# Gram products of a block computed in one go and kept in SBUF, per-couple element-wise work, expert weights applied to x, and a new instruction order

## The chip, the cores and the metric

The kernel runs on one core of a Trainium2 chip. The metric is the device time of one execution in microseconds (us), the median of three runs. One further execution was profiled; all rows below come from it, and their times count from the start of its span.

## The reference

The input x is (2 batches, 128 times, 16 bands, 64 channels). The reference first adds to x the result of six layers of a dual-path selective-state network (Mamba2) on a normed x, then adds a dense mixture of 16 experts. Each of the 12 passes (a "time" pass over t, then a "band" pass over the 16 bands, six times) computes, cut to what matters:

```python
zxbcdt = rmsnorm(x) @ Win
xBC    = silu(causal_conv4(xBC))            # xs (128), B (16), C (16)
dt     = softplus(dt + dt_bias)             # 8 heads
h_t    = exp(-dt*exp(A)) * h_{t-1} + (xs*dt) B_t ;  y_t = h_t . C_t + D*xs
x      = x + rmsnorm(y * silu(z)) @ Wout
# mixture of experts, top 2 of 16, all experts computed
out    = x + sum_e mix[:, e] * ((silu(x @ w1[e]) * (x @ w2[e])) @ w3[e])
```

The recurrence is evaluated without a scan. For a stretch of positions t and sources s it is y_t = sum_s G[s,t] * L[s,t] * dt_s * xs_s, with the Gram matrix G = B^T C, shared by the eight heads, and L = exp(cumsum differences) for each head.

## The kernel before

A pass is two blocks, one for each batch, so there are 24 blocks (k = 0 to 23), each 1024 positions with 128 inner channels. Block kind 0 is a time pass and kind 1 a band pass. A block has 8 pairs (i), two pairs make a couple (c = i // 2). In a pair the positions lie in halves of 64: kind 0 needs three (source, target) squares, LL, LH and HH; kind 1 needs two, LL and HH. All engines follow orders written out by hand, with semaphores between them; the work on block k is interleaved with the preparation of block n = k + 1.

For a pair, TensorE does these steps in order:

- `g_and_xt(n, i)`: the Gram products of the pair, from `bc` (B rows) and `cm` (C rows), 16 partitions each, into one PSUM bank `gx`, and two transposes of `xs` into the same bank. It waits for `s_w`: the weighing of the pair before must have read `gx` (lines 700 to 720).
- `mix_states(k, i)`: 32 small float32 products of `em` (weighted decays) and `xdt` into `ybank`, after `weigh(k, i)` (lines 733 to 749).
- `decays(n, i)`: the exponents L, as bf16 products of `lt` and `rt` into the ring of four PSUM banks, a bank a square (lines 722 to 731).

ScalarE takes each ring bank through `exps` (Exp) into `em`. VectorE does `x_dt` (transposed xs times dt), `weigh` (em times G, broadcast over heads, 128 x 1536 elements for kind 0, 128 x 1024 for kind 1) and `gate_y` (the skip D*xs from `ybank`, line 1252, and the gate, line 1262) for each pair, and `norm_out` for each couple. GpSimd squares the gated y for each pair (`square_y`, line 556) and adds the couple's output to x (`add_x`, line 563). `project_out(k, c)` on TensorE makes the output projection and the sum of squares.

The preparation of block n: `mean`, `project_dt`, `turn_dt`, `project_x` (8 products of 512 columns in two calls), `sum_dt`, `project_bc`, `project_z` and `turn_parts`. SyncE's queue then issues the DMAs in the order written: `c_rows(n)`, four DMAs that place the C rows (`cm`) once `bc` is ready (line 396), and `target_rows(n, 0)` and `(n, 1)`, together 12 DMAs for kind 0 and 8 for kind 1, which place rows of `rt` once `rows_of_cum` has copied the output of `turn_parts` to `lt` (line 407). `g_and_xt(n, 0)` waits for all four `cm` DMAs, `decays(n, 0)` for `target_rows(n, 0)`, and `decays(n, 4)` for `target_rows(n, 1)`. The order at the end of a block, before:

```python
# TensorE
project_x(n, 1); turn_parts(n); project_z(n, 0); project_z(n, 1)
project_out(k, 2); g_and_xt(n, 0); mix_states(k, 7); decays(n, 0); decays(n, 1)
# SyncE
c_rows(n); target_rows(n, 0); target_rows(n, 1)
```

In the expert stage there are 4 chunks of 512 columns and 16 experts, 64 steps. In each step TensorE computes h1 and h2 for two halves of the tokens (line 867), two bf16 products that spread the expert's mixing weight over the rows (line 872) and the output product (line 891). ScalarE applies Silu, and VectorE makes four products of 128 x 512: silu times h2, and that times the mixing weight, for two halves (lines 1409 and 1414).

Of the kernel before, what the change touches and what calls it, by code (L numbers as in the profile page):

```python
# [11 lines left out]
P = 128  # L12
QUAD = 32
# [71 lines left out]


def ring_turns():
# [12 lines left out]
    t.two("z", 0, 1)  # L100
    t.seg(0, 0)
    t.seg(0, 1)
    for k in range(NBLOCK):
        n = k + 1
        t.seg(k, 2)
        t.seg(k, 3)
        t.seg(k, 4)
        t.one("mean", n, 1)
# [5 lines left out]
        t.two("x", n, 0)  # L114
        t.one("cum", n)
        t.two("bc", n)
        t.two("x", n, 1)
        t.one("parts", n)
        t.two("z", n, 0)
        t.two("z", n, 1)  # L120
        t.seg(n, 0)
        t.seg(n, 1)
        t.one("mean", n + 1, 0)
    return t.turn


def build(nc, a, out):
    with ExitStack() as ctx:
# [8 lines left out]
        gx = ctx.enter_context(nc.psum_tensor("gx", [P, CK], F32))  # L137
# [3 lines left out]
        def rbank(*key):  # L141
# [53 lines left out]
        xdt = [sb(f"xdt{u}", [P, 2 * HEADS // 2, 2, 2 * HD]) for u in range(2)]  # L195
        yt = [sb(f"yt{u}", [P, 2 * T]) for u in range(2)]
# [29 lines left out]
        s_g, s_xdt, s_w, s_y, s_yf, s_yg, s_ysq = (sem(n) for n in (  # L226
            "g_and_x_turned", "xdt_ready", "weighed", "y_ready", "y_bank_read", "y_gated", "y_squared"))
# [9 lines left out]
        sil, act_h = ([emf[:, CK * (2 * k + b):CK * (2 * k + b + 1)] for b in range(2)] for k in range(2))  # L237
        hidden = [[emf[:, CK * (4 + 2 * k + b):CK * (5 + 2 * k + b)] for b in range(2)] for k in range(2)]
        moe = rstd[:, 0, :]
        xq = rstd[:, 1, :]  # L240
# [8 lines left out]
        target = [rt1[:, E * P * b:E * P * (b + 1)].rearrange("p (e t) -> p e t", e=E) for b in range(2)]  # L249
# [11 lines left out]
        s_xq, s_h1, s_h2, s_gb, s_sil, s_u, s_hid, s_eo, s_oc2, s_ot, s_acc = (sem(n) for n in (  # L261
            "xq_ready", "h1_ready", "h2_ready", "mix_spread", "silu_done", "silu_times_h2", "hidden_ready", "expert_out",
            "sum_copied", "sum_transposed", "accumulated"))
        NSTEP = 2 * E
        bank = ring + [gx, ybank[:, 0, :], ybank[:, 1, :], oss]
# [36 lines left out]
        def in_half(ap):  # L302
            return ap.rearrange("p (m w) -> p m w", w=HALF)

# [40 lines left out]
        def _(sp):  # L345
# [4 lines left out]
            def weights_in(g):  # L350
# [5 lines left out]
                if g >= 2:  # L356
                    sp.wait_ge(s_wp, g - 1)
                    sp.wait_ge(s_yg, NPAIR * 2 * (g - 1))
# [32 lines left out]
            def c_rows(n):  # L391
                sp.wait_ge(s_bc, 2 * (n + 1))
                if n >= 2:
                    sp.wait_ge(s_g, NPAIR * (n - 1))
# [24 lines left out]
            for k in range(NBLOCK):  # L419
# [11 lines left out]
            sp.wait_ge(s_yg, NPAIR * NBLOCK)  # L431
            sp.wait_ge(s_g, NPAIR * NBLOCK)
# [15 lines left out]
        def _(pool):  # L448
# [102 lines left out]
            def square_y(k, i):  # L551
                p, u = NPAIR * k + i, (i // 2) % 2
                pool.wait_ge(s_yg, p + 1)
                if p >= 4:
                    pool.wait_ge(s_o, p // 2 - 1)
                pool.tensor_tensor(out=ysq[u][:, i % 2, :], in0=yg[u][:, i % 2, :], in1=yg[u][:, i % 2, :],  # L556
                                   op=ALU.mult).then_inc(s_ysq, 1)
# [8 lines left out]
            for k in range(NBLOCK):  # L566
                for i in range(NPAIR):
                    square_y(k, i)
                    if i == 0 and k >= 1:
                        add_x(k - 1, 3)  # L570
                    if i == 3:
                        add_x(k, 0)
                    if i == 5:
                        add_x(k, 1)
                    if i == 6 and k % 2 == 0 and k >= 2 and pass_of(k) + 1 < NPASS:
                        weights_made(pass_of(k) + 1)
                add_x(k, 2)
            add_x(NBLOCK - 1, 3)
# [10 lines left out]
            for b in range(2):  # L589
                selector(pool.memset(target[b][:], 0.0))  # L590
                for r in range(NPART):
                    v = target[b][QUAD * r:QUAD * (r + 1)]
                    selector(pool.affine_select(out=v, in_=v, compare_op=ALU.not_equal, fill=1.0, base=-E * b,
                                                pattern=[[-1, E], [0, P]], channel_multiplier=1))

        @block.tensor
        def _(pe):
# [102 lines left out]
            def g_and_xt(n, i):  # L700

                p = NPAIR * n + i
                if i == 0:
                    pe.wait_ge(s_cm, 64 * (n + 1))
                    pe.wait_ge(s_xs, 4 * (n + 1))
                if p:
                    pe.wait_ge(s_w, p)
                rows = slice(QUAD * (i // 2), QUAD * (i // 2) + NST)
                b, c = (pair_of(t[n % 2][rows, :], i % 2) for t in (bc, cm))
                wide = T if kind(n) == 0 else HALF  # L710
                for ab in range(2):
                    pe.matmul(gx[HALF * ab:HALF * (ab + 1), 0:wide], b[:, 0, ab, :], c[:, 0:wide // HALF, ab, :],  # L712
                              start=True, stop=True)
                for ab in range(2):
                    pe.matmul(gx[HALF * ab:HALF * (ab + 1), wide:wide + HALF], b[:, 1, ab, :], c[:, 1, ab, :],
                              start=True, stop=True)
                for h in range(2):
                    tr = pe.transpose(gx[:, 2 * T + T * h:2 * T + T * (h + 1)],  # L718
                                      xs[n % 2][:, 2 * T * i + T * h:2 * T * i + T * (h + 1)], ident[:])
                tr.then_inc(s_g, 1)  # L720
# [12 lines left out]
            def mix_states(k, i):  # L733
                p = NPAIR * k + i
                pe.wait_ge(s_w, p + 1)
                if p:
                    pe.wait_ge(s_yf, p)
                wide = T if kind(k) == 0 else HALF
                for first in (0, 1):
                    lo, hi = (0, wide) if first == 0 else (wide, wide + HALF)  # L740
                    for r in range(2):
                        for q in range(HEADS // 2):
                            for ab in range(2):
                                rows = slice(HALF * ab, HALF * (ab + 1))
                                o = ybank[QUAD * q:QUAD * (q + 1), ab, (HALF if first else 0):(T if first else wide)]
                                mm = pe.matmul(o, xdt[p % 2][rows, 4 * first + q, r, :],  # L746
# [4 lines left out]
            def project_out(k, c):  # L751
                u, m = pass_of(k) % 2, 4 * k + c
                pe.wait_ge(s_ysq, NPAIR * k + 2 * c + 2)
# [24 lines left out]
            g_and_xt(0, 0)  # L778
# [3 lines left out]
            for k in range(NBLOCK):  # L782
                n = k + 1
                more = n < NBLOCK
                g_and_xt(k, 1)
                mix_states(k, 0)
                decays(k, 2)
                if k:
                    project_out(k - 1, 3)
                g_and_xt(k, 2)  # L790
                mix_states(k, 1)
                decays(k, 3)
                g_and_xt(k, 3)
                mix_states(k, 2)
                decays(k, 4)
                if more:
                    mean(n, 1)
                g_and_xt(k, 4)
                mix_states(k, 3)
                decays(k, 5)  # L800
                project_out(k, 0)
                if more:
                    project_dt(n)
                g_and_xt(k, 5)
                mix_states(k, 4)
# [3 lines left out]
                project_out(k, 1)  # L809
                g_and_xt(k, 6)  # L810
                mix_states(k, 5)
                decays(k, 7)
                if more:
                    project_x(n, 0)
                    sum_dt(n)
                    project_bc(n)
                g_and_xt(k, 7)
                mix_states(k, 6)
                if more:
                    project_x(n, 1)  # L820
                    turn_parts(n)
                    project_z(n, 0)
                    project_z(n, 1)
                project_out(k, 2)
                if more:
                    g_and_xt(n, 0)
# [30 lines left out]
            pe.wait_ge(s_sel, 2 * (1 + NPART))  # L857

            def chunk(q, first=False):
                def experts_in(e):  # L860
                    again = e >= 1 or not first
                    for w, k, used in ((w1s, 0, s_sil), (w2s, 1, s_u)):
                        for b in range(2):
                            if again:
                                pe.wait_ge(used, NSTEP * q + 2 * e + b - 1)
                            rows = slice(C * b, C * b + C)
                            pe.matmul(bank[2 * b + k][:], w[rows, e, :], xq[rows, :],  # L867
                                      start=True, stop=True).then_inc((s_h1, s_h2)[k], 1)
                    for b in range(2):
                        if again:  # L870
                            pe.wait_ge(s_hid, NSTEP * q + 2 * e + b - 1)
                        pe.matmul(bank[4 + b][:], target[b][0:NPART * QUAD, e, :],
                                  cum_t[0:NPART * QUAD, 4 * q:4 * q + 4, :].rearrange("k j t -> k (j t)"),
# [573 lines left out]
```

## Time and profile before

| | us |
|---|---|
| median of 3 runs (lowest to highest) | 1425.25 (1423.16 to 1425.64) |
| the profiled execution, its device time | 1429.27 |
| its span | 1427.5 |
| TensorE matrix products, busy | 1201.1 (84%) |
| VectorE, busy | 906.4 (63%) |
| ScalarE, busy | 721.5 (51%) |
| GpSimd, busy | 274.0 (19%) |
| mean granted TensorE clock | 0.953 of 2.4 GHz |

The profile lists, for each group of instructions, the line of the kernel, the engine, what is written and read, the busy time and the idle time before it with what ended it. TensorE's weight loads (PEld) overlap its matrix products (PE). A float32 product shows as two instructions. A span differs from the device time of its execution by what lies before the first and after the last instruction.

### The profile page before, as it was taken

How to read it: one execution, taken by the hardware profiler on the slowest of the kernel's cores; microseconds unless marked ns; L12 is line 12 of the kernel's file. 1: busy time of each engine (PE TensorE's matmuls, PEld its weight loads, DVE VectorE, ACT ScalarE, POOL GpSimd, SP SyncE). 2: the span in 40 equal slices, each digit the busy share in tenths (PEclk: the TensorE clock that was granted, in tenths of full speed). 3: DMA queues.
4: the chain of work that ended last, by engine and by line, in shares of the span. 5: the costliest groups of instructions: out<-in, count | busy, mean ns of one | idle time of the engine just before them, and what ended most of it. 6: DMA issues, size and time to landing. Idle time of an engine off the chain costs nothing. (4 is left out here: it accounts for less than half of the span.)

```text
span 1427.5 us, 47284 instructions
## 1 busy us (share of the span) xinstructions
PE 1201.1 (84%) x20280; PEld 629.2 (44%) x20280; DVE 906.4 (63%) x1667; ACT 721.5 (51%) x1358; POOL 274.0 (19%) x406
## 2 busy tenths in 40 slices
PE   2698888888888889888888888888888835999998
PEld 1354444544444544444544445445444432333332
DVE  4466655765566655765566655766566657777776
ACT  3356556565656655565556655566556411333332
POOL 7211121211211212212121121222212250000000
PEclk9699999989999999999999999999999957999999
DMA  3100000100011000110001100011000040000000
GB/s 74 23 7 7 23 14 21 36 7 22 10 23 34 11 11 20 22 36 10 9 21 20 36 14 8 22 20 30 20 7 5 9 74 0 1 9 0 8 8 8
DMA packets 69600, 26.45 MB, mean 19 GB/s; under 512 B 54928, under 2 KB 66320, under 8 KB 69392
## 3 DMA queue, kind: packets, MB, share of 16 engines
q1 hardware_dynamic: 69392, 23.42, 8.2%
q8 instruction: 161, 2.64, 0.8%
q14 instruction: 47, 0.39, 0.1%
HBM read 9.96 MB, written 1.05 MB: 8 GB/s over the span
## 5 line engine op out<-in xcount | busy, mean ns | idle before, releaser
L977 ACT ACTIVATE em<-ring 128x512 f32<-128x512 f32 x480 | 255.3, 599 | 245.7 <-PE ring L729 245.5
L1244 DVE TENSOR_TENSOR em<-em,gx 128x1536 f32<-128x1536 f32 (+1 forms) x192 | 283.5, 1477 | 29.6 <-ACT em L977 29.6
L556 POOL TENSOR_TENSOR ysq<-yg 128x256 f32<-128x256 f32 x192 | 117.9, 614 | 871.6 <-DVE yg L1262 871.6
L746 PE MATMUL ybank<-em,xdt 64*32 64x64 f32 (+1 forms) x12288 | 189.2, 242 | 1.0 <-issue 0.4
L746 PEld LDWEIGHTS ybank<-em,xdt 64*32 64x32 f32 x12288 | 156.5, 107 | 35.6 <-issue 34.7
L729 PE MATMUL ring<-rt,lt 128*64 128x512 bf16 x960 | 149.7, 413 | 15.6 <-DMA rt<-lt 10.6
L712 PE MATMUL gx<-cm,bc 16*64 16x128 f32 (+1 forms) x768 | 74.6, 270 | 91.2 <-DVE em L1244 82.7
L1110 ACT ACTIVATE em<-ring 128x512 f32<-128x512 f32 x128 | 69.6, 594 | 147.3 <-PE ring L867 147.2
L996 ACT ACTIVATE xs<-ring,col 128x512 f32<-128x512 f32 x96 | 60.8, 684 | 152.2 <-PE ring L671 152.2
L712 PEld LDWEIGHTS gx<-cm,bc 16*64 16x64 f32 x768 | 37.5, 131 | 194.7 <-DVE em L1244 165.6
L1270 DVE TENSOR_TENSOR on<-oss,rr 128x256 f32<-128x256 f32 x96 | 40.1, 418 | 124.4 <-ACT rr L987 124.2
L1252 DVE SCALAR_TENSOR_TENSOR yt<-xs,col,ybank 128x128 f32<-128x128 f32 x384 | 114.9, 340 | 0.0
L1409 DVE TENSOR_TENSOR em<-em,ring 128x512 f32<-128x512 f32 x128 | 87.5, 684 | 42.2 <-PE ring L867 42.2
L1234 DVE TENSOR_TENSOR xdt<-gx,dt 128x256 f32<-128x256 f32 x192 | 80.3, 418 | 32.4 <-PE gx L718 32.0
L671 PE MATMUL ring<-h_t,wt 64*128 64x512 f32 x384 | 92.2, 618 | 0.8 <-ACT em L977 0.7
L671 PE MATMUL ring<-h_b,wt 64*128 64x512 f32 x384 | 91.3, 613 | 1.1 <-ACT em L977 1.1
L718 PE MATMUL gx<-ident,xs 128*128 128x128 f32 x384 | 86.2, 307 | 0.0
L1262 DVE TENSOR_TENSOR yg<-yt,zs 128x256 f32<-128x256 f32 x192 | 81.6, 425 | 6.6
L623 PE MATMUL ring<-xsq,mean 128*128 128x512 f32 x96 | 55.3, 660 | 23.0 <-ACT xsq L938 22.8
L867 PE MATMUL ring<-rstd,xs 64*128 64x512 f32 x256 | 73.2, 649 | 0.8 <-DVE lt L1394 0.8
L891 PE MATMUL ybank<-em,w3s 128*64 128x512 f32 x256 | 69.0, 618 | 1.5 <-DVE em L1414 1.5
L757 PE MATMUL oss<-yg,wo 128*64 128x256 f32 x384 | 61.1, 395 | 9.8 <-PE ring L681 7.8
(168 smaller groups left out, 1655.1 us busy)
## 6 DMA issues: line engine op xcount, KB each, us to landing
x_b<-x_t SPq DMA_DIRECT2D x48, 128.0 KB, 3.0
rt<-lt SPq DMA_DIRECT2D x240, 12.0 KB
cm<-bc SPq DMA_DIRECT2D x96, 32.0 KB, 2.0
cw<-in_L_conv_t_cw SPq DMA_DIRECT2D x6, 320.0 KB
cw<-in_L_conv_b_cw SPq DMA_DIRECT2D x6, 320.0 KB
x_in<-in_x SPq DMA_DIRECT2D x4, 256.0 KB, 4.2
xs<-in_L_ffn_w SPq DMA_DIRECT2D x2, 512.0 KB, 7.0
zs<-in_L_ffn_w SPq DMA_DIRECT2D x2, 512.0 KB, 9.2
```

The source lines that it names most:

```text
L556: pool.tensor_tensor(out=ysq[u][:, i % 2, :], in0=yg[u][:, i % 2, :], in1=yg[u][:, i % 2, :], op=ALU.mult).then_inc(s_ysq, 1)
L671: mm = pe.matmul(o[half], wt[u][rows, k, 0:DIN], conv_in(n, half, k, 4 * c, 4), start=(k == 0), stop=(k == DCONV - 1))
L712: pe.matmul(gx[HALF * ab:HALF * (ab + 1), 0:wide], b[:, 0, ab, :], c[:, 0:wide // HALF, ab, :], start=True, stop=True)
L718: tr = pe.transpose(gx[:, 2 * T + T * h:2 * T + T * (h + 1)], xs[n % 2][:, 2 * T * i + T * h:2 * T * i + T * (h + 1)], ident[:])
L729: mm = pe.matmul(o[HALF * ab:HALF * (ab + 1), :].rearrange("p (h t) -> p h t", h=HEADS), lt[:, n % 2, ab, i, :], rt[i // 4][:, blk, :, i % ...
L746: mm = pe.matmul(o, xdt[p % 2][rows, 4 * first + q, r, :], em[rows, p % EM_SLOTS, 2 * q + r, lo:hi], start=(first == 0 and r == 0), stop=( ...
L977: emptied(act.activation(em[:, p % EM_SLOTS, :, HALF * j:HALF * (j + 1)], o.rearrange("p (h t) -> p h t", h=HEADS), ACT.Exp), "seg", n, i, ...
L1234: dve.tensor_tensor(v, gx[:, 2 * T:4 * T].rearrange("p (k r d) -> p k r d", r=2, d=HD), dt[n % 2][:, 16 * i:16 * (i + 1)].rearrange("p (k ...
L1244: dve.tensor_tensor(e, e, gx[:, 0:wide].rearrange("p (o t) -> p o t", o=1).to_broadcast([P, HEADS, wide]), ALU.mult).then_inc(s_w, 1)
L1252: ins = dve.scalar_tensor_tensor(out=pair_of(yt[p % 2][:], 0)[:, :, ab, :], in0=pair_of(xs[k % 2][:], i)[:, :, ab, :], scalar=col[u][:, D_ ...
L1262: dve.tensor_tensor(yg[c % 2][:, i % 2, :], yt[p % 2][:], zs[k % 2][:, 2 * T * i:2 * T * (i + 1)], ALU.mult).then_inc(s_yg, 1)
L1409: dve.tensor_tensor(act_h[b], sil[b], bank[2 * b + 1][:], ALU.mult).then_inc(s_u, 1)
```

## The change

In the blocks:

- The Gram products of all eight pairs come in one call, `gram(n)`, into four ring banks, a bank a couple. The couples' rows lie in the four 32-partition quadrants, and the inner loop runs over them. ScalarE copies the banks to a new SBUF tensor `gs` (`copy_gram`), and `weigh` reads `gs`. `gram(n)` waits for the four `cm` DMAs.
- `turn_x(n, c)` transposes xs by couple into a bank of its own (`xtb`), and `x_dt`, the skip (`add_skip`), the gate and `square_y` work by couple, with instructions twice as long and half as many.
- All orders are new. On TensorE `mix_states(k, 5)` to `(k, 7)` and `project_out(k, 1)` move into the preparation of block n, `project_bc` moves behind `project_z(n, 0)`, and `turn_parts` behind `project_z(n, 1)`. On SyncE's queue `target_rows` now stand ahead of `c_rows`.

In the expert stage the mixing weight is applied to x ahead of the product with w2 (`weigh_x`) and not to the product: a step has one bf16 spreading product in place of two, and three products on VectorE in place of four. `xq` and its copy go.

```diff
@@ SyncE
                     if kind(n) == 0:
                         cross(n)
-                    c_rows(n)
                     target_rows(n, 0)
                     target_rows(n, 1)
+                    c_rows(n)
@@ TensorE
-            def g_and_xt(n, i):
-
-                p = NPAIR * n + i
...
-                if p:
-                    pe.wait_ge(s_w, p)
...
+            def gram(n):
+
+                pe.wait_ge(s_cm, 64 * (n + 1))
+                o = [take("gram", n, j) for j in range(4)]
                 wide = T if kind(n) == 0 else HALF
...
+                for u in range(2):
+                    at = (wide + HALF) * u
+                    for half in range(2):
+                        lo, hi = (0, wide) if half == 0 else (wide, wide + HALF)
+                        for ab in range(2):
+                            for j in range(4):
+                                rows = slice(QUAD * j, QUAD * j + NST)
+                                b, c = (pair_of(t[n % 2][rows, :], u) for t in (bc, cm))
+                                mm = pe.matmul(o[j][HALF * ab:HALF * (ab + 1), at + lo:at + hi], b[:, half, ab, :],
+                                               c[:, half:(wide // HALF if half == 0 else 2), ab, :],
+                                               start=True, stop=True)
...
@@ ScalarE
+            def copy_gram(n):
+                w = HALF * len(BLOCKS[kind(n)])
+                for j in range(4):
+                    o = filled("gram", n, j)
+                    if n >= 2:
+                        act.wait_ge(s_w, NPAIR * (n - 2) + 2 * j + 2)
+                    emptied(act.activation(gs[n % 2][:, 2 * j:2 * j + 2, 0:w], o[:, 0:2 * w].rearrange(
+                        "p (u t) -> p u t", u=2), ACT.Copy), "gram", n, j)
...
@@ VectorE, weigh
-                dve.tensor_tensor(e, e, gx[:, 0:wide].rearrange("p (o t) -> p o t", o=1).to_broadcast([P, HEADS, wide]),
+                dve.tensor_tensor(e, e, gs[n % 2][:, i:i + 1, 0:wide].to_broadcast([P, HEADS, wide]),
                                   ALU.mult).then_inc(s_w, 1)
@@ TensorE, expert stage
+            def spread_mix(k):
+
+                if k >= 2:
+                    pe.wait_ge(s_xm, k - 1)
+                pe.matmul(bank[4 + k % 2][:], target[0][0:NPART * QUAD, k % E, :],
+                          cum_t[0:NPART * QUAD, 4 * (k // E):4 * (k // E) + 4, :].rearrange("k j t -> k (j t)"),
+                          start=True, stop=True).then_inc(s_gb, 1)
...
@@ VectorE, expert stage
+            def weigh_x(k):
+                dve.wait_ge(s_gb, k + 1)
+                if k >= 2:
+                    dve.wait_ge(s_h2, 2 * k - 2)
+                dve.tensor_tensor(xm[k % 2], x2[:, CK * (k // E):CK * (k // E) + CK], bank[4 + k % 2][:],
+                                  ALU.mult).then_inc(s_xm, 1)
```

TensorE's order in a block after the change, several calls to a line:

```python
turn_x(k, 1); project_out(k - 1, 3); decays(k, 2); mix_states(k, 0)
mix_states(k, 1); decays(k, 3); turn_x(k, 2); mean(n, 1)
decays(k, 4); turn_x(k, 3); mix_states(k, 2); decays(k, 5)
mix_states(k, 3); project_dt(n); decays(k, 6); turn_dt(n)
project_out(k, 0); decays(k, 7); mix_states(k, 4)
project_x(n, 0); project_out(k, 1); project_x(n, 1); sum_dt(n)
mix_states(k, 5); project_z(n, 0); project_bc(n); project_z(n, 1)
turn_parts(n); project_out(k, 2); mix_states(k, 6)
gram(n); turn_x(n, 0); mix_states(k, 7)
decays(n, 0); decays(n, 1); mean(n + 1, 0)
```

## Rows read from the trace of the kernel before

**Rows 1.** Windows: all 24 blocks, then part of the expert stage.
```profile
core 0: us, PE busy (x) PEld busy (x) DVE busy (x) ACT busy (x) POOL busy (x), PEclk, DMA share, GB/s
60.00:1137.00 1077.00, 931.20 (x18968) 524.07 (x18970) 668.96 (x1319) 621.53 (x1181) 218.84 (x322) 0.97 0.09 18
```

**Rows 2.** Windows of the expert stage, columns as in rows 1.
```profile
1196.00:1300.00 104.00, 104.00 (x418) 34.72 (x415) 78.49 (x119) 33.78 (x62) 0.00 (x0) 0.99 0.02 3
```

**Rows 3.** Windows: four block-to-block stretches, each from a `project_x(n, 0)` to the next.
```profile
410.70:458.00 47.30, 41.20 (x816) 23.25 (x815) 29.96 (x58) 28.69 (x55) 8.55 (x12) 0.99 0.14 30
458.00:508.50 50.50, 43.70 (x814) 24.78 (x816) 31.49 (x57) 28.48 (x56) 11.10 (x16) 0.94 0.03 8
508.50:553.20 44.70, 39.36 (x796) 21.39 (x794) 25.80 (x55) 24.42 (x47) 7.78 (x12) 0.92 0.09 19
553.20:594.80 41.60, 36.18 (x797) 19.96 (x795) 25.91 (x57) 24.68 (x48) 10.84 (x16) 1.00 0.11 21
```

**Rows 4.** Timeline of TensorE, n of kind 0: start, us, what, idle before.
```profile
467.42 3.70 PE L671 MATMUL ring<-h_t,wt 64*128 64x512 f32 x16
471.06 0.63 PE L662 MATMUL ring<-identb,parts 128*64 128x128 bf16 x8
...
478.08 2.06 PE L729 MATMUL ring<-rt,lt 128*64 128x512 bf16 x12 [0.89 <-DMA rt<-lt]
...
482.01 0.43 PE L712 MATMUL gx<-cm,bc 16*64 16x128 f32 x4
...
482.49 0.44 PE L718 MATMUL gx<-ident,xs 128*128 128x128 f32 x2
482.86 1.05 PE L746 MATMUL ybank<-em,xdt 64*32 64x128 f32 x64
...
496.07 0.60 PE L757 MATMUL oss<-yg,wo 128*64 128x256 f32 x4
```

**Rows 5.** Timeline of SyncE's queue: n of kind 0, then the next, kind 1.
```profile
466.66 2.50 SPq L396 DMA_DIRECT2D cm<-bc  x4
472.17 9.47 SPq L407 DMA_DIRECT2D rt<-lt  x12
...
521.41 6.09 SPq L407 DMA_DIRECT2D rt<-lt  x8
```

**Rows 6.** Tile cm: time from a DMA's issue to its landing.
```profile
DMA to landing us min/median/max: 1.9/2.0/3.2
```

**Rows 7.** The page's costliest groups: the Gram products, idle before them last.
```profile
L712 PE MATMUL gx<-cm,bc 16*64 16x128 f32 (+1 forms) x768 | 74.6, 270 | 91.2 <-DVE em L1244 82.7
```

**Rows 8.** Windows around an idle stretch of TensorE, columns as in rows 1.
```profile
532.00:534.00 2.00, 0.58 (x8) 0.13 (x6) 2.00 (x4) 1.45 (x4) 0.00 (x0) 1.00 0.03 4
...
540.00:542.00 2.00, 2.00 (x4) 0.50 (x2) 0.53 (x2) 0.87 (x2) 0.61 (x1) 0.50 0.02 0
```

**Rows 9.** Timeline of TensorE: one `mix_states` just after 1.69 us idle.
```profile
505.29 1.61 PE L746 MATMUL ybank<-em,xdt 64*32 64x128 f32 x64
```

**Rows 10.** Timeline of VectorE and GpSimd, three places.
```profile
488.13 1.74 DVE L1244 TENSOR_TENSOR em<-em,gx 128x1536 f32<-128x1536 f32 x1
488.19 0.73 POOL L563 TENSOR_TENSOR x_b<-on,x_b 128x256 f32<-128x256 f32 x1
...
575.26 0.87 POOL L563 TENSOR_TENSOR x_t<-on,x_b 128x256 f32<-128x256 f32 x1
575.50 1.18 DVE L1162 TENSOR_TENSOR h_t<-x_t,rstd 128x512 f32<-128x512 f32 x1 [0.89 <-ACT rstd L946]
...
585.59 0.69 DVE L1162 TENSOR_TENSOR h_t<-x_t,rstd 128x512 f32<-128x512 f32 x1 [1.25 <-ACT rstd L946]
```

**Rows 11.** Timeline of TensorE in the expert stage: one step.
```profile
1323.76 0.39 PE L872 MATMUL gx<-lt,rt 96*128 96x512 bf16 x1
...
1324.30 1.08 PE L891 MATMUL ybank<-em,w3s 128*64 128x512 f32 x4
...
1327.22 0.39 PE L872 MATMUL gx<-lt,rt 96*128 96x512 bf16 x1
```

More of the change, by code:

```diff
@@ L84, in two, with four @@
             self.take(name, n, c, 1)
+    def four(self, name, n):
+        if n < NBLOCK:
+            for j in range(4):
+                self.take(name, n, j)
 def ring_turns():
@@ L100, in ring_turns @@
     t.two("z", 0, 1)
+    t.four("gram", 0)
     t.seg(0, 0)
@@ L106, in ring_turns @@
         t.seg(k, 3)
+        t.one("mean", n, 1)
         t.seg(k, 4)
-        t.one("mean", n, 1)
         t.seg(k, 5)
@@ L114, in ring_turns @@
         t.two("x", n, 0)
+        t.two("x", n, 1)
         t.one("cum", n)
+        t.two("z", n, 0)
         t.two("bc", n)
-        t.two("x", n, 1)
+        t.two("z", n, 1)
         t.one("parts", n)
-        t.two("z", n, 0)
-        t.two("z", n, 1)
+        t.four("gram", n)
         t.seg(n, 0)
@@ L777, in _ @@
             project_z(0, 1)
-            g_and_xt(0, 0)
+            gram(0)
+            turn_x(0, 0)
             pe.wait_ge(s_rep, 12)
@@ L808, in _ @@
                     turn_dt(n)
-                project_out(k, 1)
-                g_and_xt(k, 6)
-                mix_states(k, 5)
+                project_out(k, 0)
                 decays(k, 7)
+                mix_states(k, 4)
                 if more:
                     project_x(n, 0)
+                project_out(k, 1)
+                if more:
+                    project_x(n, 1)
                     sum_dt(n)
+                mix_states(k, 5)
+                if more:
+                    project_z(n, 0)
                     project_bc(n)
-                g_and_xt(k, 7)
+                    project_z(n, 1)
+                    turn_parts(n)
+                project_out(k, 2)
                 mix_states(k, 6)
                 if more:
[L820 to L826, printed above, removed]
+                    gram(n)
+                    turn_x(n, 0)
                 mix_states(k, 7)
@@ L856, in _ @@
             pe.wait_ge(s_gc, 2)
[L857 to L873, printed above, removed]
-                                  start=True, stop=True).then_inc(s_gb, 1)
-                pe.wait_ge(s_xq, q + 1)
-                for e in range(E):
-                    experts_in(e)
-                    if e >= 1:
-                        expert_out(q, e - 1, first)
-                    elif not first:
-                        expert_out(q - 1, E - 1, False)
-                    if e == 1 and not first:
-                        sum_to_tokens(q - 1)
@@ L886, in expert_out @@
[L886 to L888 removed]
+            pe.wait_ge(s_sel, 1 + NPART)
+            def spread_mix(k):
[4 more added lines that the diff above has]
+                          start=True, stop=True).then_inc(s_gb, 1)
@@ L1334, in _ @@
                 norm_out(k, 2)
-            gate_y(NBLOCK - 1, 7)
+                if more:
+                    x_dt(n, 0)
+                add_skip(k, 3)
+                gate_y(k, 3)
             norm_out(NBLOCK - 1, 3)
```

353 lines of the change are left out of this document (179 added, 174 removed).

## Prediction

> **What bounds the kernel now.** I read the windows first. The 24 blocks fill the stretch from 60 to 1137 us; in these 1077 us TensorE is busy for 931.2, VectorE for 669 and ScalarE for 622 [rows 1]. The expert stage is TensorE's alone: 104.00 of 104 us busy [rows 2]. In four blocks taken one by one TensorE works 41.2 of 47.3, 43.7 of 50.5, 39.4 of 44.7 and 36.2 of 41.6 us [rows 3]. So TensorE's own work is some 87% of a block, and the 146 us that it idles over all blocks are the rest. The reader should see that no other engine is above 63% of a block, so that a shorter VectorE or ScalarE instruction pays only where TensorE stands waiting for it.
>
> What TensorE waits for is in the groups with their idle time: 82.7 of the 146 us are spent ahead of the Gram products, until VectorE's `weigh` has read the one bank `gx` [rows 7]. The timeline of a handover shows the rest of the shape: after `turn_parts` at 471.06 comes work until the decays of the next block, which start at 478.08 after 0.89 us of waiting for a DMA [rows 4]. That DMA is the last of the first half of `target_rows`: SyncE's queue issued the four `cm` DMAs from 466.66, ahead of and beside TensorE's work, and the twelve `rt` DMAs from 472.17 over 9.47 us [rows 5]. The chain from `turn_parts` through SyncE's queue is thus already just longer than its cover.
>
> **The change, part by part.**
>
> *Gram products.* One pair's products take from 482.01 to 482.49, 0.48 us [rows 4], 3.8 us a block of kind 0, and about 3.0 for kind 1, whose first product has half the columns. In one call they are 64 small instructions in quadrants and column halves. The nearest row is `mix_states`, 64 such instructions in 1.05 us [rows 4]. I take 1.1 us; the bounds are 1.0, and 3.8 if quadrants do not overlap. That takes off 2.7 and 1.9 us. The transposes stay in number (eight pairs of two become four runs of four), and I take 0.5 us a block for hand-overs between groups that go, with bounds 0 and 1. Together 2.8 us a block on average, 67 us.
>
> *The wait for `gx`.* It goes, and with it the 82.7 us. VectorE and ScalarE also get room: longer instructions, half as many. ScalarE gains four copies; no row of the blocks stands for them, and I take 2 us a block, with bounds 0 and 3, on an engine that is busy for 28.5 of 50.5 us [rows 3]. They stand ahead of `exps(n, 0)` and TensorE has transposes, `mix_states(k, 7)` and decays to do meanwhile. If that cover were gone they would cost 1.5 us a block.
>
> *The order on SyncE's queue.* This is the part that decides. `gram(n)` waits for all four `cm` DMAs, and these now stand behind all of `target_rows`, which cannot be issued before `turn_parts` is done and copied. Ahead of everything else stands TensorE's own order: behind the waiting `gram(n)` are `turn_x(n, 0)`, `mix_states(k, 7)` and all decays of block n, so ScalarE's exps and VectorE's weighing wait too. The chain, from the start of `turn_parts`: 1.1 us to the first `rt` issue (471.06 to 472.17 [rows 4, 5]); 9.1 us for twelve issues (this row is a long one with 9.47, most of its eleven like have 9.07) or 6.1 for eight (6.09 [rows 5]); 1.9 us until the fourth `cm` issue (three quarters of 2.50 [rows 5]); 2.0 us to its landing [rows 6]. That is 14.1 us for kind 0 and 11.1 for kind 1. Beside it TensorE has `turn_parts` (0.6), `project_out(k, 2)` (two groups like that of 496.07, some 1.0) and `mix_states(k, 6)` (1.0, or 0.8 in kind 1) [rows 4]: 2.6 and 2.4. TensorE stands still for 11.5 us in each of 11 handovers to kind 0 and for 8.7 us in each of 12 to kind 1: 126 + 104 = 231 us. In the kernel before, `cm` was issued first and hidden under `project_x(n, 1)`; nothing in the new order can hide it, since the earliest that `bc` is ready is two calls ahead of `turn_parts`.
>
> *Idle time that stays.* Of the old 146 us I keep 1.0 us a block, 24 us, for ring banks not yet read by ScalarE and for weighing that is late behind the stall; bounds 0 and 3 us a block.
>
> *The clock.* After the window 532 to 534, in which TensorE worked 0.58 of 2 us, the granted clock is 1.00 still in that window and 0.50, the lower level (1.2 GHz), at 540 to 542 [rows 8]; after 1.69 us idle a `mix_states` took 1.61 us and not 1.05 [rows 9, 4]. Stalls of 9 to 12 us will end at the lower level every time. Of the work behind them (`gram`, transposes, `mix_states(k, 7)`, first decays) I let some 4 us run at about 1.6 times its time: 1.7 us a handover, 39 us. The blocks now lose some too (mean clock 0.97 [rows 1]), about half of which goes with the short waits; net 22 us, bounds 0 and 60.
>
> *GpSimd and the shared memory.* `weigh` had one operand in PSUM; now both are in SBUF. The timeline shows what that may mean. A `weigh` of 1.74 us and a GpSimd addition of 0.73 us ran side by side at their usual lengths (488.13 and 488.19). But the product of x and rstd, both in SBUF, took 1.18 us when it began inside a GpSimd addition (575.50, the addition from 575.26 for 0.87) and 0.69 when none ran (585.59) [rows 10]. Each block has eight GpSimd operations (then of double length for the squares), three of which start just ahead of a `weigh`: after `gate_y(k, 0)`, `(k, 1)` and `norm_out(k, 0)`. I count 0.3 us a block of this as part of the 1.0 above, since VectorE has slack there. The Trainium skill, "SBUF — State Buffer", section "SBUF: two separate sides", says that a Vector operation with two SBUF inputs and a GpSimd operation that reads SBUF take an exclusive lock, so that the later one is blocked for the whole of the earlier; by that rule the new `weigh` collides and the old did not, and the rows at 488 and 575 agree.
>
> *Expert stage.* A step takes 3.46 us (1323.76 to 1327.22), and the two spreading products 0.54 of it (to 1324.30) [rows 11]. Half goes: 0.26 x 64 = 17 us. h2 now needs the weighted x, computed a step ahead; VectorE has one product of 128 x 512 less a step. TensorE stays the bound, so these change nothing. Bounds 10 and 25 us.
>
> **The sum.** Blocks: 931 - 67 + 231 + 24 + 22 = 1141 against 1077, so 64 us more. Experts: 17 less. The span goes from 1427.5 to about 1474.5, its execution from 1429.3 to 1476. The median of the runs is 4 us below the profiled execution, so the median to expect is 1472.
>
> **Rivals.**
>
> - *The forecast*: the stall behind `target_rows`. Chance 0.63; 1450 to 1500.
> - *The order of issue does not bind* (faster). If the 9 us that SyncE's queue shows did not hold back the next DMA, `cm` would land as soon as `bc` is ready, and the stall would be at most about 2 us: 1472 - 23 x 8 = 1288. For it speaks only that a busy queue is no proof of a blocked one; against it, that the first decays wait for a DMA just when six issues in a row and a landing are through: the sixth starts at 472.17 + 5 x 0.79 = 476.1 and lands 2.0 later at 478.1, and they began at 478.08 [rows 4 to 6]. The whole change turns faster once the mean wait is under 8 us a handover and not 10, with the other terms as taken. Chance 0.09 for a result faster by over 0.2%, which is about what a measurement of this kernel can tell.
> - *No change*: the stall as said, but every other wait and the cold clock gone: 931 - 67 + 231 = 1095, 18 more, less 17. Chance 0.05.
> - *The lock on weighing*. All eight GpSimd operations of a block delay VectorE or are delayed, and 1.7 us more a block come on the path: 24 x 1.7 = 41, 1513. Chance 0.09.
> - *The Gram products do not overlap*: they stand on the path at every handover with 3.8 or 3.0 us: 23 x 2.3 = 53, 1525. Chance 0.06.
> - *A longer cold clock*: 7 us and not 4 behind each stall, 1.5 x 23 = 35, 1507. Chance 0.08.
>
> The range 1438 to 1516 takes in the forecast, the longer cold clock, the lock and the lower bounds of idle and clock together in part; about 2 in 10 are left out. Slower has 0.86, same 0.05, faster 0.09.
>
> **What would show it.** In the profile after, TensorE's idle time ahead of the Gram products must be put down to the DMA `cm<-bc`, over 200 us in 23 waits, and SyncE's timeline must show twelve or eight `rt` issues, then four `cm`. The granted clock must be near 0.5 behind each. The Gram group of a block should take 1.1 us at the full clock, up to 2 behind a stall. `weigh` rows well above 1.74 us in kind 0 would show the lock. Steps of the expert stage should take 3.2 us. The prediction is wrong if `cm` lands early, or if the work behind a stall is not the old work in a shorter time but waits anew for VectorE.

## The result, and the profile after

The changed kernel takes 1495.84 us (median of 4 runs, 1489.65 to 1499.44) against 1424.2 us for the kernel before (4 runs). The ratio is 1.0504, with a 95% interval of 1.0461 to 1.0546: slower by 5.0%, in the forecast's direction and inside its range of 1438 to 1516, 24 us above the 1472 that it named.

First the page of the changed kernel, busy times and TensorE's clock over 40 slices:

```profile
PE 1133.8 (76%) x20216; PEld 587.1 (39%) x20216; DVE 842.3 (56%) x1219; ACT 761.6 (51%) x1450; POOL 315.1 (21%) x306
...
PEclk8789888988898889888988899888988875899999
```

TensorE works 67 us less than before and VectorE 64 us less, and yet the span is 67 us longer. The clock is below full in nearly every slice of the blocks. The windows that answer to [rows 1, 3], first all blocks, then three stretches from one `project_x(n, 0)` to the next:

```profile
61.40:1209.10 1147.70, 871.44 (x18849) 488.14 (x18847) 646.72 (x935) 661.76 (x1274) 263.20 (x226) 0.87 0.08 17
...
423.70:475.60 51.90, 39.65 (x878) 22.57 (x876) 28.05 (x42) 31.11 (x60) 10.52 (x9) 0.87 0.08 18
475.60:528.90 53.30, 39.77 (x822) 22.51 (x812) 29.64 (x41) 30.57 (x60) 13.39 (x13) 0.87 0.09 18
528.90:574.40 45.50, 35.08 (x771) 19.59 (x763) 26.93 (x41) 25.75 (x50) 10.03 (x9) 0.89 0.07 18
```

The blocks take 1147.7 us in place of 1077, with 871 of TensorE's work in place of 931: its idle time has gone from 146 to 276 us. The waits within the blocks say for what:

```profile
DVE xdt L1265 <- PE xtb L737: 275.2, 24, 13.8
ACT gs L1059 <- PE ring L725: 247.9, 24, 12.6
...
PE ring L725 <- DMA cm<-bc: 238.2, 23, 12.2
```

238 of the 276 us stand ahead of the Gram products, in 23 waits for the DMA that places the C rows; VectorE and ScalarE wait behind it, for the same 23 handovers and the first. One handover to a block of kind 0 on TensorE (start, us, what, idle before), which answers to [rows 4]:

```profile
489.90 0.55 PE L674 MATMUL ring<-identb,parts 128*64 128x128 bf16 x7 [0.34 <-PE ring L693]
...
491.31 1.05 PE L768 MATMUL ybank<-em,xdt 64*32 64x128 f32 x64
504.41 1.71 PE L725 MATMUL ring<-cm,bc 16*64 16x128 f32 x64 [12.05 <-DMA cm<-bc]
506.05 1.11 PE L737 MATMUL xtb<-ident,xs 128*128 128x128 f32 x4
507.09 1.61 PE L768 MATMUL ybank<-em,xdt 64*32 64x128 f32 x64
508.63 2.68 PE L748 MATMUL ring<-rt,lt 128*64 128x512 bf16 x12
```

And SyncE's queue at this handover and the next, of kind 1, against [rows 5]:

```profile
490.99 9.10 SPq L419 DMA_DIRECT2D rt<-lt  x12
500.20 2.75 SPq L408 DMA_DIRECT2D cm<-bc  x4
544.13 6.09 SPq L419 DMA_DIRECT2D rt<-lt  x8
550.33 2.47 SPq L408 DMA_DIRECT2D cm<-bc  x4
```

The reader should put the two side by side: `turn_parts` starts at 489.90, the first `rt` issue follows 1.1 us later, twelve issues take 9.1 us, then come the four `cm` issues, and TensorE starts again at 504.41, 14.5 us after `turn_parts`. The `rt` rows, for which `decays(n, 0)` waited before, have long landed by then.

### The profile page after: what moved, and what is told of

It is laid out like the page before. It is cut to its first block, busy times and chain, and to the rows that moved or that the text cites. A ratio compares the mean times of both kernels' runs of the same rounds, so it can differ in the third digit from the quotient of the medians.

```text
span 1494.5 us, 46811 instructions
## 1 busy us (share of the span) xinstructions
PE 1133.8 (76%) x20216; PEld 587.1 (39%) x20216; DVE 842.3 (56%) x1219; ACT 761.6 (51%) x1450; POOL 315.1 (21%) x306
## 4 chain that ended last, share of the span: by engine, by line
PE 61%; SPq 13%; issue 9%; DVE 7%; DMA 3%; POOL 3%; ACT 2%; POOLq 0%; ACTq 0%; DVEq 0%
PE ring L683 12%; SPq L419 10%; PE ybank L768 8%; PE ring L895 5%; PE ring L748 4%; PE ybank L910 4%; PE ring L901 4%; PE ring L693 3%; DMA cm<-bc 3%; PE ring L707 3%; SPq L408 3%; PE xtb L737 3%; PE ring L725 2%; PE oss L780 2%; PE ring L635 2%
## 5 line engine op out<-in xcount | busy, mean ns | idle before, releaser
L1276 DVE TENSOR_TENSOR em<-em,gs 128x1536 f32<-128x1536 f32 (+1 forms) x192 | 325.0, 1712 | 12.6 <-ACT em L1006 11.9
L568 POOL TENSOR_TENSOR ysq<-yg 128x512 f32<-128x512 f32 x96 | 128.1, 1334 | 738.3 <-DVE yg L1296 738.3
L1265 DVE TENSOR_TENSOR xdt<-xtb,dt 128x512 f32<-128x512 f32 x96 | 65.4, 681 | 275.2 <-PE xtb L737 275.2
L1283 DVE SCALAR_TENSOR_TENSOR yt<-xs,col,ybank 128x256 f32<-128x256 f32 x192 | 83.2, 474 | 29.1 <-PE ybank L768 28.9
L1014 ACT ACTIVATE rr<-oss,eps 128x256 f32<-128x256 f32 x96 | 45.5, 474 | 88.3 <-PE oss L783 86.4
L748 PEld LDWEIGHTS ring<-rt,lt 128*64 128x64 bf16 x960 | 48.2, 117 | 81.0 <-issue 45.0
L575 POOL TENSOR_TENSOR x_b<-on,x_b 128x256 f32<-128x256 f32 x48 | 61.0, 1270 | 85.4 <-DVE on L1304 85.2
L575 POOL TENSOR_TENSOR x_t<-on,x_b 128x256 f32<-128x256 f32 x48 | 56.8, 1183 | 84.4 <-DVE on L1304 84.4
L737 PE MATMUL xtb<-ident,xs 128*128 128x128 f32 x384 | 73.2, 322 | 0.3 <-DVE xdt L1265 0.3
L895 PE MATMUL ring<-xs 64*128 64x512 f32 x256 | 73.2, 649 | 0.0
```

Of the source, the lines that this page charges most:

```text
L568: pool.tensor_tensor(out=ysq[c % 2][:], in0=yg[c % 2][:], in1=yg[c % 2][:], op=ALU.mult).then_inc(s_ysq, 1)
L575: pool.tensor_tensor(out=couple_to(k, c), in0=in_couple(k, on[c % 2][:]), in1=couple_from(k, c), op=ALU.add).then_inc(s_x, 1)
L737: tr = pe.transpose(xtb[:, T * i:T * (i + 1)], xs[n % 2][:, T * (4 * c + i):T * (4 * c + i + 1)], ident[:])
L748: mm = pe.matmul(o[HALF * ab:HALF * (ab + 1), :].rearrange("p (h t) -> p h t", h=HEADS), lt[:, n % 2, ab, i, :], rt[i // 4][:, blk, :, i % ...
L895: pe.matmul(bank[2 * b][:], w1s[rows, e, :], x2[rows, cols], start=True, stop=True).then_inc(s_h1, 1)
L1276: dve.tensor_tensor(e, e, gs[n % 2][:, i:i + 1, 0:wide].to_broadcast([P, HEADS, wide]), ALU.mult).then_inc(s_w, 1)
```

## The experiments

Eight kernels, each timed against the kernel before on the same chip.

**The order on SyncE's queue, put back** (the changed kernel with one edit):

```diff
                     if kind(n) == 0:
                         cross(n)
+                    c_rows(n)
                     target_rows(n, 0)
                     target_rows(n, 1)
-                    c_rows(n)
```

> The changed kernel with one edit: c_rows(n) ahead of target_rows(n, 0) and (n, 1) in SyncE's queue, as in the kernel before. My theory (the cm DMAs stand behind the rt DMAs): the 245 us of TensorE idle ahead of gram falls to under 50, and the wait moves to the first decays, which then need bc, four cm issues (2.5 us), six or four rt issues and a landing; the handover is 8.5 to 10 us shorter than in the changed kernel, the clock mostly stays up; 1260 to 1300 us. Rival (the new orders on the other engines or the Gram copies on ScalarE set the time): the idle only moves to ScalarE or VectorE and the time stays above 1450. Rival (the lock between weigh and GpSimd sets the block): about 1420 or more.

Measured: 1295.01 us, ratio 0.9079 (0.9039 to 0.9119) to the kernel before. One line of order is worth 201 us. Its queue and its TensorE at one handover, then its blocks:

```profile
418.55 3.35 SPq L408 DMA_DIRECT2D cm<-bc  x4
422.00 9.49 SPq L419 DMA_DIRECT2D rt<-lt  x12
```

```profile
423.36 1.10 PE L725 MATMUL ring<-cm,bc 16*64 16x128 f32 x64 [1.94 <-DMA cm<-bc]
424.39 0.66 PE L737 MATMUL xtb<-ident,xs 128*128 128x128 f32 x4
424.98 1.05 PE L768 MATMUL ybank<-em,xdt 64*32 64x128 f32 x64
427.93 2.28 PE L748 MATMUL ring<-rt,lt 128*64 128x512 bf16 x12 [1.90 <-DMA rt<-lt]
```

```profile
60.00:1004.00 944.00, 844.80 (x18849) 468.87 (x18847) 640.75 (x935) 661.61 (x1273) 263.93 (x226) 0.97 0.10 21
```

The wait for `cm` is 1.94 us here and not 12.05 (over the blocks 42.3 us in 23 waits and not 238.2), a wait of 1.90 us for `rt` appears as expected, and the mean clock in the blocks is back at 0.97. The rivals in which ScalarE, VectorE or the lock bounds the block are out.

**The same order in the kernel before** (`c_rows(n)` behind both `target_rows`):

```diff
-                    c_rows(n)
                     target_rows(n, 0)
                     target_rows(n, 1)
+                    c_rows(n)
```

> The kernel before with one edit: c_rows(n) behind target_rows(n, 0) and (n, 1). My theory: g_and_xt(n, 0) begins when cm has landed, 14.1 us (kind 0) or 11.1 us (kind 1) after the start of turn_parts, in place of 4.2 us, so some 8 us more in each of 23 handovers with the colder clock: 1424 + 23 x 8 to 9 = 1608 to 1630 us. Rival (SyncE's issues do not hold each other back): no change, 1424.

Measured: 1645.18 us, ratio 1.1537 (1.1486 to 1.1589), 15 us above the top of what was expected. The wait appears in the old Gram products:

```profile
PE gx L712 <- DMA cm<-bc: 199.7, 24, 10.3
```

In the profiled executions, 224 us apart, the wait for `cm` grew by 193 us (6.5 to 199.7), TensorE's busy time by 60 us (1201.1 to 1261.1, at a mean granted clock of 0.879 and not 0.953), and its other idle time fell by 29 us. The order costs 218 us in this kernel and 201 us in the changed one, so its price is about the same in both, and what the change brings apart from it is some 130 us.

**The expert stage alone** (the kernel before with `spread_mix`, `weigh_x` and the new loops of the expert stage):

```diff
-                    for b in range(2):
...
-                        pe.matmul(bank[4 + b][:], target[b][0:NPART * QUAD, e, :],
+                pe.matmul(bank[4 + k % 2][:], target[0][0:NPART * QUAD, k % E, :],
```

> The kernel before with the new expert stage alone (one spreading product a step, mixing weight on x). The forecast's term: 64 x 0.26 = 17 us less, 1407 us, a step of 3.2 us and not 3.46. Rival (the shorter VectorE chain or a lost cover changes the step otherwise): outside 1400 to 1414. Also told apart: whether the gating products with gate_w take 4.0 us as before or 6.9 us as in the changed kernel.

Measured: 1410.5 us, ratio 0.9901 (0.9866 to 0.9936), 16 us less than its 1426.8 of before. The gating products took 3.8 us; where the 6.9 us of the changed kernel come from is told further down.

**Gram products by couple** (the changed kernel with `for j in range(4)` outermost in `gram`, so that neighbours share a quadrant):

```diff
-                for u in range(2):
+                for j in range(4):
+                    for u in range(2):
...
-                            for j in range(4):
```

> The changed kernel with the loop over the couples outermost in gram, so that neighbouring products lie in one quadrant of rows and only the two column halves can overlap. If the four quadrants are what makes gram short: the gram group takes over 3 us and not 1.7 or 1.3, it stands on the path after each stall, less what ScalarE's earlier first copy gives back: 1496 + 23 x 1 to 2.5 = 1520 to 1550. If only leaving out the waits made it short: within 5 us of 1496.

Measured: 1530.66 us, ratio 1.0734 (1.0704 to 1.0765), 35 us above the changed kernel. The group behind the stall:

```profile
517.95 3.66 PE L725 MATMUL ring<-cm,bc 16*64 16x128 f32 x64 [12.05 <-DMA cm<-bc]
```

3.66 us and not 1.71, the same 64 instructions after the same idle time; for kind 1 it is 2.60 us and not 1.29. Over the 23 handovers that is 37 us more work, of which 35 came on the path, 1.5 us each. So the order of the inner loop is what makes `gram` short. The edit changes two things at once, though: neighbouring products share a quadrant of rows and also write the same PSUM bank, where in the changed kernel they go round four quadrants and four banks. Which of the two counts was not told apart.

**TensorE kept busy in the stall**: extra bf16 products, whose results nobody reads, ahead of the wait.

```diff
+                if n:
+                    for i in range(90 if kind(n) == 0 else 62):
+                        pe.matmul(ybank[:, 1, 2 * T:4 * T], identb[:], rtmpl[:, 0, :, :].rearrange(
+                            "p h t -> p (h t)")[:, 0:2 * T], start=True, stop=True)
                 pe.wait_ge(s_cm, 64 * (n + 1))
```

> The changed kernel with TensorE kept busy in the stall: 90 (kind 0) or 62 (kind 1) extra bf16 products of 256 columns on constants, written to columns of ybank that nobody reads, ahead of the wait for cm. The stall itself stays. Theory (the lower clock behind each stall is on the path): gram, transposes, mix_states(k, 7) and first decays take 4.2 us and not 6.8, so 1.5 to 2.6 us a handover, 1436 to 1462 us. Rival (the work behind the stall waits for ScalarE and VectorE anyway): within 10 us of 1496. If the extra products outlast the stall, more than 1496.

Measured: 1481.83 us, ratio 1.0407 (1.0369 to 1.0445), 14 us below the changed kernel. That is between the theories. Two handovers, the first of kind 0:

```profile
485.80 10.00 PE L716 MATMUL ybank<-rtmpl,identb 128*128 128x256 bf16 x90
498.65 1.71 PE L729 MATMUL ring<-cm,bc 16*64 16x128 f32 x64 [2.85 <-DMA cm<-bc]
...
538.53 6.94 PE L716 MATMUL ybank<-rtmpl,identb 128*128 128x256 bf16 x62
547.35 0.91 PE L729 MATMUL ring<-cm,bc 16*64 16x64 f32 x64 [1.88 <-DMA cm<-bc]
```

In the first the Gram products took 1.71 us as in the changed kernel, in the second they ran at full speed. These two do not stand for all 23 handovers, in which the fill left 1.83 to 2.96 us idle. In 8 of them the mean granted clock of the 8 us from the start of `gram` stayed at 1.00; in the other 15 it fell, mostly only after the Gram products. The length of the idle rest alone does not tell which: these two windows (columns as in [rows 1]) both stand behind 1.83 us of it.

```profile
692.76:700.76 8.00, 7.15 (x160) 4.36 (x162) 4.86 (x6) 6.14 (x12) 1.04 (x1) 1.00 0.02 4
886.03:894.03 8.00, 7.83 (x158) 4.92 (x160) 4.64 (x6) 5.92 (x12) 1.04 (x1) 0.79 0.01 2
```

So the first fill kept the clock up in part of the handovers only, and I filled the rest, with `range(112 if kind(n) == 0 else 78)`:

> As e5_filled, which left some 2 us of idle ahead of each gram, with 112 (kind 0) or 78 (kind 1) extra products, so that they end within a few tenths of the landing of cm. Theory (the lower clock is on the path and costs 1.5 to 2.6 us a handover where it holds): the granted clock stays at 1.00 in every handover, gram at 1.1 or 0.9 us, and the time goes to 1440 to 1470, below the 1482 of e5_filled. Rival (e5_filled has taken all that was on the path; the rest is behind ScalarE): 1475 to 1485.

Measured: 1466.68 us, ratio 1.0292 (1.0269 to 1.0315), 29 us below the changed kernel.

```profile
483.22 12.40 PE L716 MATMUL ybank<-rtmpl,identb 128*128 128x256 bf16 x112
495.55 1.10 PE L729 MATMUL ring<-cm,bc 16*64 16x128 f32 x64
496.58 0.66 PE L741 MATMUL xtb<-ident,xs 128*128 128x128 f32 x4
```

No work was removed, the added products are of no use, and 29 us are gone. The stall is as long as before (`turn_parts` at 480.83, `gram` at 495.55, 14.7 us); only what follows it is faster. The clock of the 8 us from the start of `gram` is 1.00 in all 23 handovers. The rival in which the first fill had taken all that was on the path is out.

**GpSimd reads no SBUF** (the kernel of the first experiment with the squares and the additions to x replaced by memsets):

```diff
-                pool.tensor_tensor(out=ysq[c % 2][:], in0=yg[c % 2][:], in1=yg[c % 2][:], op=ALU.mult
-                                   ).then_inc(s_ysq, 1)
+                pool.memset(ysq[c % 2][:], 1.0).then_inc(s_ysq, 1)
...
-                pool.tensor_tensor(out=couple_to(k, c), in0=in_couple(k, on[c % 2][:]), in1=couple_from(k, c),
-                                   op=ALU.add).then_inc(s_x, 1)
+                pool.memset(couple_to(k, c), 1.0).then_inc(s_x, 1)
```

> The kernel e1_rows_first with GpSimd's squares and additions to x replaced by memsets of the same tiles: left out are the squares and the residual sums, GpSimd reads no SBUF in the blocks. Theory (weigh with both operands in SBUF and GpSimd's reads exclude each other, and it costs time in this kernel): weigh falls from a mean of 1.92 to 1.74 us (kind 0) and from 1.44 to 1.21 (kind 1), 1.4 to 1.9 us a block on VectorE; if that is on the path 1250 to 1270. Rival (VectorE has slack, TensorE bounds the block): the rows fall as said but the time stays within 12 us of 1295.

Measured: 1282.48 us, ratio 0.8994 (0.8963 to 0.9025), 12.5 us below the 1295.01 of its base. The groups of `weigh` in it, in kind 0 and kind 1:

```profile
L1274 DVE TENSOR_TENSOR em<-em,gs 128x1536 f32<-128x1536 f32 x96 | 166.3, 1753 | 26.4 <-ACT em L1004 26.4
...
L1274 DVE TENSOR_TENSOR em<-em,gs 128x1024 f32<-128x1024 f32 x96 | 115.1, 1220 | 4.5 <-ACT em L1004 3.7
```

The rows are at 1.75 and 1.22 us, against 1.92 and 1.44 in its base, and so back at their lengths in the kernel before (1.74 and 1.21). The collision is thus shown, and it comes from the reads: the memsets still write SBUF for 80 us in all, and the rows carry nothing of it. The time lies between the theory's 1250 to 1270 and the rival's 12 us, half a microsecond outside the latter: `weigh` in all got 37 us shorter and the kernel 12.5, so VectorE's slack takes most of it. The 12.5 us are an upper bound, since the memsets are also shorter than what they replace, and the runs of the two kernels spread over 9 and 12 us.

**B and C rows earlier** (the kernel of the first experiment; ring turns and ScalarE's order follow the same sequence):

```diff
                 project_out(k, 1)
                 if more:
-                    project_x(n, 1)
-                    sum_dt(n)
+                    project_bc(n)
                 mix_states(k, 5)
                 if more:
+                    sum_dt(n)
+                    project_x(n, 1)
+                    turn_parts(n)
                     project_z(n, 0)
-                    project_bc(n)
                     project_z(n, 1)
-                    turn_parts(n)
```

> The kernel e1_rows_first with project_bc straight behind project_out(k, 1), then mix_states(k, 5), sum_dt, project_x(n, 1), turn_parts, and both project_z (ring turns and ScalarE's order to match), so that the cm DMAs are issued under project_x(n, 1) and the rt DMAs start two calls earlier. Theory: gram waits for nothing (49 us of idle go) and the wait of the first decays for rt (17 us) shrinks under 15, the clock stays up: 1225 to 1250. Rival (ring banks or VectorE become the wait ahead of project_x(n, 1) and turn_parts): 1270 to 1300.

Measured: 1283.38 us, ratio 0.9002 (0.898 to 0.9023), the fastest kernel of this study that leaves nothing out, 10% faster than the kernel before, but not the 1225 to 1250 of the theory.

```profile
60.00:1000.00 940.00, 835.07 (x18920) 476.70 (x18922) 643.01 (x937) 658.02 (x1275) 267.30 (x227) 0.99 0.10 21
```

The clock is at 0.99, and TensorE's idle time in the blocks is 105 us, hardly more than the 99 of the first experiment's window. The waits for the DMAs went, and others came in their place; two of them, in one preparation:

```profile
408.29 0.46 PE L662 MATMUL ring<-dta,tri_time 128*128 128x128 f32 x2 [0.41 <-ACT xs L1025]
...
409.52 3.70 PE L683 MATMUL ring<-h_t,wt 64*128 64x512 f32 x16 [0.60 <-ACT bc L1047]
```

Both are ring banks that ScalarE has not read yet, as the rival said; over the blocks they come to 10.8 and 15.9 us, 23 waits each, and the first experiment had neither. The gain is in the work itself at the higher clock, 835.1 us and not 844.8; the idle time did not fall.

## Why the prediction was right, and where it was off

**The step that decided.** The chain through SyncE's queue was given as 14.1 us for kind 0 and 11.1 for kind 1, and the stall as 11.5 and 8.7. Measured: 12.05 us in the handover shown, and 238 us in 23 waits against 231. The first two experiments change nothing but the order of these calls and move the time by 201 and 218 us, so that the cause is shown and not only argued. The rival in which the issues do not hold each other back is out. This step was right in mechanism and in size.

**The terms.** The span grew by 67 us, where 47 were forecast:

| term, us | forecast | measured |
|---|---|---|
| stall ahead of `gram` | +231 | +238 |
| TensorE's busy time in the blocks, clock included | -67 + 22 | -60 (931 to 871) |
| idle time that stays | 24 in place of 146 | 38 (1147.7 - 871.4 - 238.2) |
| blocks together | +64 | +71 |
| expert stage | -17 | -17 |
| end of the blocks to the first w1 product | 0 | +11.4 |
| start | 0 | +1.4 |

The blocks together came near the forecast because errors of opposite sign met: 7 us more stall and 14 us more of the other idle time (0.6 us a block), against 15 us less busy time. That is luck. The first experiment takes the busy time apart, since its blocks make the same products at the clock of the kernel before (0.97): 844.8 us. So the work itself fell by 86 us (931.2 to 844.8), where 67 were taken, and the lower clock added 27 (844.8 to 871.4), where 22 were taken. The mis-sized term is the Gram products with the transposes: they kept TensorE busy for 168.0 us before and for 91.4 in the first experiment, 77 less, where 55 were taken. The Gram products are there at 25.1 us, as forecast (24 x 1.1); the gain that was missed is in the transposes, whose change the forecast put at nothing because their number stays. They take 66.3 us there, against some 86 before (168.0 less the products as the forecast read them, 3.8 and 3.0 us a block).

**What was left out.** The forecast had no term for the end of the blocks. From the last decays to the first product with w1 it is 59.2 us before and 70.6 after. In block 23 there is no next block to prepare, so nothing lies beside the serial chain from y to x; with couples in place of pairs the chain has fewer and longer links. TensorE there, in the changed kernel:

```profile
1216.94 0.65 PE L780 MATMUL oss<-yg,wo 128*64 128x256 f32 x4 [4.25 <-POOL ysq L568]
...
1223.05 1.12 PE L780 MATMUL oss<-yg,wo 128*64 128x256 f32 x4 [2.81 <-POOL ysq L568]
```

It waits for squares of a whole couple. This part is about 8 us (11.5 us from the last decays to GpSimd's first selector before, 19.7 after); that the couples are the reason is argued from these rows and not tried. Another 1.0 us are the two first spreading products, which now stand ahead of the first w1 product, and a wait between is 0.6 us shorter. The last 2.9 us are the clock's. The gating products took 4.0 us before and 6.9 here, and the windows around them, before and after, show the granted clock (last column but two):

```profile
1169.50:1173.50 4.00, 3.98 (x33) 3.87 (x32) 0.74 (x2) 0.00 (x0) 0.00 (x0) 0.91 0.02 4
...
1249.20:1256.10 6.90, 6.84 (x33) 6.71 (x32) 0.76 (x3) 0.00 (x0) 0.00 (x0) 0.50 0.00 0
```

Both stand behind some 15 us of idle time and the same 3.7 us of transposes. In the changed kernel the clock then stayed at 0.50 for all of them; in the first experiment, with the same instructions there, they took 3.9 us. Of the ten profiles two have 6.9 us (this one and that of the kernel in which GpSimd reads no SBUF) and eight have 3.8 to 4.1. What decides between the two was not tried.

The last part of the distance between 1472 and 1496 is 3.3 us of spread between runs: the forecast took 4 us off the profiled execution to get the median, and the changed kernel's median is only 0.7 us below its own.

**The clock.** The forecast took 1.7 us a handover and 39 us in all before what the shorter waits give back. The full fill gives 29 us, 1.3 a handover; but in the profiled executions 2.8 of the 28.1 us between the two spans are the gating products just told, and 25.1 us lie up to the last Gram products (at 1191.76 and at 1166.64 us), so the price of a handover is nearer 1.1. Windows behind the stall (us, busy and count of PE, PEld, DVE, ACT, POOL, clock, DMA share, GB/s):

```profile
500.00:504.00 4.00, 0.00 (x0) 0.00 (x0) 0.00 (x0) 0.00 (x0) 0.00 (x0) 0.50 0.17 41
504.00:506.00 2.00, 1.59 (x64) 1.52 (x64) 0.00 (x0) 0.00 (x0) 0.00 (x0) 0.50 0.00 0
...
510.00:512.00 2.00, 2.00 (x10) 0.70 (x7) 1.36 (x2) 2.00 (x5) 1.04 (x1) 0.73 0.00 0
512.00:514.00 2.00, 2.00 (x17) 1.19 (x17) 2.00 (x2) 1.86 (x4) 0.00 (x0) 1.00 0.00 0
```

It is at 0.50 from the stall until past 510, some 7 us and not the 4 that the forecast gave it. The other handovers have less: 0.50 in the first 3 us behind each, then a mean of 0.59 to 0.88 over the next 5, which makes 4.2 to 7.1 us at the lower level. So the condition of the rival with 1507 us came in part and its price did not: the later part of that work is covered by ScalarE. In the fully filled kernel TensorE's waits in the blocks for ring banks that ScalarE still has to read are 12.7 us; in the changed kernel they are 1.1.

**Gram products.** Taken as 1.1 us at full clock and up to 2 behind a stall; 1.10 and 1.71 measured. The rival without overlap had 2.3 us a handover; the order without it costs 1.5.

**The lock.** The groups that answer to [rows 10], in the changed kernel:

```profile
L1276 DVE TENSOR_TENSOR em<-em,gs 128x1536 f32<-128x1536 f32 x96 | 184.7, 1943 | 10.8 <-ACT em L1006 10.4 <-issue 0.4
...
L1276 DVE TENSOR_TENSOR em<-em,gs 128x1024 f32<-128x1024 f32 x96 | 140.3, 1482 | 1.8 <-ACT em L1006 1.5
...
L575 POOL TENSOR_TENSOR x_b<-on,x_b 128x256 f32<-128x256 f32 x48 | 61.0, 1270 | 85.4 <-DVE on L1304 85.2
L575 POOL TENSOR_TENSOR x_t<-on,x_b 128x256 f32<-128x256 f32 x48 | 56.8, 1183 | 84.4 <-DVE on L1304 84.4
```

All `weigh` together went from 283.5 to 325.0 us, and a mean addition to x from 0.81 (x_b) and 0.91 (x_t) to 1.27 and 1.18. One place where both meet:

```profile
515.75 1.43 POOL L575 TENSOR_TENSOR x_b<-on,x_b 128x256 f32<-128x256 f32 x1 [4.29 <-DVE on L1304]
516.57 2.22 DVE L1276 TENSOR_TENSOR em<-em,gs 128x1536 f32<-128x1536 f32 x1
```

The product starts within the addition, with 0.61 us of it left, and takes 2.22 us in place of 1.74, 0.48 more. The rule of the Trainium skill, "SBUF — State Buffer", section "SBUF: two separate sides", on a Vector operation with two SBUF inputs and a GpSimd operation that reads SBUF agrees, from both sides: moving G from PSUM to SBUF brought the collision, and taking GpSimd's reads away ended it. The forecast put 0.3 us a block of it on the path; the experiment bounds it at 12.5 / 24 = 0.5, in the kernel without the stall. VectorE's 1.7 us a block (41.5 / 24) are mostly covered, so the rival with 1513 us did not come. That the rival named the same 1.7 us is luck, for the forecast gave no working for it.

**Expert stage.** A step, from one spreading product to the next, against 3.46 us in [rows 11]:

```profile
1422.80 0.39 PE L885 MATMUL ybank<-lt,rt 96*128 96x512 bf16 x1
...
1426.05 0.39 PE L885 MATMUL xtb<-lt,rt 96*128 96x512 bf16 x1
```

3.25 us, 0.21 less where 0.26 was taken; over 64 steps that is 13 us of the 16 to 17 that the stage lost. Of the rest 1.0 us are the two spreading products that now stand ahead of the stage's first product, and 1.0 us is a shorter wait for VectorE before the last output product (1.45 before, 0.42 after); what is left was not followed.

## What to carry to other kernels

When the consumer of a DMA moves ahead of another consumer on its engine, its issue must move on the DMA queue too: here a queue of 12 (in kind 1, 8) small DMAs at 0.76 us each stood ahead of the four that TensorE needed first, and turned a change worth a 9% gain into a 5% loss. Work out from each queue's rows when the last DMA that an engine waits for is issued, not only whether it is small. And before copying a PSUM operand to SBUF to free a bank, look at what GpSimd reads meanwhile.

## What the runs showed of the hardware that was not expected

- Filling an idle stretch with products that nobody needs made the kernel 29 us (1.9%) faster: the granted clock behind it stayed at its upper level (2.4 GHz) in all 23 handovers. A fill that left 1.83 to 2.96 us idle kept it in 8 of 23 and gave 14 us; 1.83 us of idle time stood ahead of a handover that kept it and of one that did not.
- The gating products, 6.9 us of unbroken work behind 3.65 us more of it and 14.62 us of idle time, ran at the lower clock (0.50) to their end in two profiles, and took 3.8 to 4.1 us in eight others.
- 64 matrix instructions (32 float32 products) with 16 rows each take 3.66 us when neighbours share a quadrant of rows and a PSUM bank and 1.71 us when they go round the four of each, both at the lower clock.
- A `weigh` of kind 0 with both operands in SBUF takes 1.92 to 1.94 us on average and 1.75 us when GpSimd reads no SBUF; with the second operand in PSUM it took 1.74 us beside GpSimd's reads.
